# A two-layer graph network on one core: the product with the kept probabilities waits group by group, and the first step's features are added by POOL

## The chip, the cores and the metric

The kernel is one program on one core of one Trainium2 chip. The metric is the device time of one execution in microseconds (us); where several runs of a kernel are given, the median is taken. Five engines work side by side: PE (TensorE: matmuls and turns of tiles), DVE (VectorE), ACT (ScalarE), POOL (GpSimd) and SP (SyncE, which here only issues DMAs). They meet through semaphores alone: an engine that waits stops in its own order of instructions, and everything behind the waiting instruction stops with it.

## What is computed

The input is x of 3327 x 256 and an adjacency matrix of 3327 x 3327. A first layer normalises x and averages it over neighbours. A second layer takes two diffusion steps. What matters here is the second layer:

```python
Rf = S / S.sum(axis=1);  Rb = S / S.sum(axis=0)      # S = adj + I
Xf, Xb, Xa = (X, X, X);  Z = 0
for s in range(2):
    A = adj_from_feats(Xa, W1, W2, W3)    # softmax of Xa W1 W2 (Xa W3)^T, cut to the top 0.9 of
                                          # each row's mass, and softmax again
    Xf = Rf @ Xf;  Xb = Rb @ Xb;  Xa = A @ Xa
    Z = Z + (Xf @ U1[s] + Xb @ U2[s] + Xa @ U3[s])
Y = X + Z                                 # then layer norm, gamma, beta, and the residual
```

So Y begins with X: the features are added once, in the first step (s = 0); the second step adds to what the first left.

## The kernel before

The 3327 rows are 26 tiles of 128 (NT = 26, the last one partly filled). After the first layer the kernel makes two passes, s = 0 and s = 1, here called the first and the second pass. Each goes over the 26 tiles, and a step t of a pass handles one tile of rows. The engines run their own loops and are staggered:

- **DVE** (`step`, from L1376) selects: it evaluates cuts over the 3327 exponentials of tile t (L1150), copies logits of later tiles out of PSUM (L1135), ranks the candidates (L1280 to L1310), and raises a flag for each row whose ranking was not enough (`astray`, L1310). The flags of 128 rows must come into one row to be reduced. SP does that with a small DMA to `flags_row` (L455). Meanwhile DVE writes the first half of the kept values into `window` (L1331), then waits for the DMA, reduces the flags (L1406), writes the second half (L1331), and computes kept_inv (L1457), on which `probs_ready` is set. If a row was flagged, a longer loop runs first.
- **PE** (`step`, from L884) first computes early logits of tile t + 2 (L860; they need `q_tile`, which SP loads), then waits for `probs_ready`, turns `window` in seven groups (L894, P_GROUPS: six of 4 tiles and one of 2) through two PSUM banks, with late logits in between, multiplies the turned groups in `probs_t` with the features `xcur` into `pv_ps` (L903), turns the diffused features (L909), runs the diffusion of tile t + 1 (L880), in which at k = 20 it turns the kept features `ht` (L868), projects the next queries and keys in the first pass (L825), and updates y: in the first pass the features enter `pv_ps` through a product with the identity (L920), in the second pass the y of the first enters in the same way (L923), and then twelve matmul instructions add the three products with U (L926). The end of L926 sets `y_done`.
- **ACT** moves the turned groups from PSUM to `probs_t` (L702, sets `p_moved`), computes exponentials and the first cuts of tile t + 2 (L649 to L678), scales `pv_ps` into `ht` (L711), writes the diffused features to `xfb` and `both` (L689 to L694), and copies `pv_ps` to `y_tile` (L731, sets `y_out`). In the first pass it stores `y_tile` to `y_dram` (the scratch y_scratch) itself, right behind the copy (L733), and waits for the store of the step before ahead of the next copy.
- **POOL** in the passes does only `low_parts` (L536): per step of the first pass one subtraction of 128 x 512.
- **SP** (`load`, L450) does for each step, in this order: the two halves of `q_tile` for tile t + 2 (after logits t), the flags of step t (after DVE's flag), the S tile of step t + 1, and in the second pass the y tile, after `y_done[1]`.

Several semaphores start above zero (`free_slots`): `y_done` and `y_out` at 1, `fb_ready` at 1, `lo_ready` at 1, `s_done` at 2. So in the second pass SP's wait for `y_done[1] >= t + 1` asks for the update of step t - 1.

The wait that the first part of the change splits is one line ahead of the product: `pe.wait_ge(p_moved[s], (t + 1) * NG)`, with NG = 7. Ahead of the flips of group g >= 2, PE already waits until group g - 2 is moved, since the PSUM bank is needed again.

Of the kernel before, what the change touches and what calls it, by code (L numbers as in the profile page):

```python
# [13 lines left out]
P = 128  # L14
N = 3327
D = 256
# [60 lines left out]
def graph_layers(nc, x, adj, w0, b0, w1, w2, w3, u1, u2, u3, gamma, beta, out):  # L77
    ctx = ExitStack()
    with ctx:
# [219 lines left out]
        s_done = [sem(f"s_done_{n}") for n in range(2)]  # L299
        fb_ready = [sem(f"fb_ready_{n}") for n in range(2)]  # L300
        fb_turned = [sem(f"fb_turned_{n}") for n in range(2)]
        lo_ready = [sem(f"lo_ready_{n}") for n in range(2)]
        logits_used = [sem(f"logits_used_{n}") for n in range(2)]
        p_flipped = [sem(f"p_flipped_{n}") for n in range(2)]
# [37 lines left out]
        def tile_of(m, b):  # L342
            return m + HALF_T * b
# [43 lines left out]
        def _(sp):  # L387
# [44 lines left out]
            for s in range(2):  # L432
                def load_q(m, b):
                    for h in range(2):
                        sp.dma_start(q_tile[b][DA * h:DA * (h + 1), :], dram_tile(q_dram[s], tile_of(m, b))).then_inc(q_in[s][b], DMA)
                if s == 0:
                    for b in range(2):
                        sp.wait_ge(team_stored[b], DMA * stores_of(NTEAM + (NTEAM + b) % 2))
                else:
                    sp.wait_ge(q_stored[1], DMA * (NT + 1))  # L440
                for b in range(2):
                    load_q(0, b)

                def load_s(t, m, b):
                    sp.wait_ge(s_done[s], t + 1)
                    sp.dma_start(flat(s_tile[b][:, :, :]), dram_tile(s_dram, tile_of(m, b))).then_inc(s_in[s][b], DMA)

                load_s(0, 0, 0)

                def load(t, m, b):  # L450
                    if not (isinstance(t, int) and t >= NT - 2):
                        sp.wait_ge(logits_ready[s], (t + 1) * NL)
                        load_q(m + 1, b)
                    sp.wait_ge(flags_ready[s], t + 1)
                    sp.dma_start(flags_row, astray[:, :]).then_inc(flags_in[s], DMA)  # L455
                    if not is_last(t):
                        load_s(t + 1, m + b, 1 - b)
                    if s == 1:
                        sp.wait_ge(y_done[1], t + 1)
                        sp.dma_start(y_in[:, :], dram_tile(y_dram, tile_of(m, b))).then_inc(y_loaded[1], DMA)  # L460
                tiles_loop(sp, load)
                if s == 0:

                    for b in range(2):
                        sp.wait_ge(xa_stored[0][b], DMA * (NT // 2 + 1))
                    sp.wait_ge(y_stored[0], DMA * (NT + 1))
                    sp.wait_ge(y_done[0], NT + 1)
                    sp.dma_start(xcur[:, :, :], xa_dram.rearrange("t p d -> p t d")).then_inc(xa_in, DMA)
                    load_u(1)
# [11 lines left out]
        def _(pool):  # L481
# [54 lines left out]
            def low_parts(t, m, b):  # L536
                pool.wait_ge(fb_ready[0], t + 2)
                G.tensor_tensor(tile4(both, tile_of(m, b), 1), xfb[:, :], tile4(both, tile_of(m, b), 0), ALU.subtract).then_inc(lo_ready[0], 1)
            tiles_loop(pool, low_parts)

        @block.scalar
        def _(act):
# [99 lines left out]
            for s in range(2):  # L642
# [54 lines left out]
                def step(t, m, b):  # L697
                    more = not (isinstance(t, int) and t >= NT - 2)

                    for g, (k0, n) in enumerate(P_GROUPS):  # L700
                        act.wait_ge(p_flipped[s], t * NG + g + 2)
                        A.activation(probs_t[:, k0 * P:(k0 + n) * P], flip_ps[g % 2][:, 0:n * P], ACT.Copy).then_inc(p_moved[s], 1)  # L702

                    if more:
                        exponentials(t + 2, b)
                        refine(b, 0)

                    act.wait_ge(pv_done[s], t + 1)
                    if s == 0:
                        act.wait_ge(xa_stored[0][b], DMA * (m + 1))  # L710
                    A.activation(ht[b][:, :], pv_ps[:, 0:D], ACT.Copy, scale=kept_inv[b]).then_inc(xa_ready[s], 1)  # L711
                    if more:
                        refine(b, 1)
                    act.drain()
                    act.wait_ge(fb_turned[s], t + 2)
                    if s == 0:
                        act.wait_ge(xa_ready[0], t + 3)
                        act.dma_start(dram_tile(xa_dram, tile_of(m, b)), ht[b][:, :]).then_inc(xa_stored[0][b], DMA)
                    act.wait_ge(x_turned[s], t + 1)
                    A.activation(flat(xfbt[:, :, :]), flip_ps[1][:, :], ACT.Copy)  # L720
                    A.activation(flat(xt[:, :, :]), pv_ps[:, D:2 * D], ACT.Copy).then_inc(x_t_ready[s], 1)
                    if s == 0:
                        query_key(t, m, b)
                    if not is_last(t):
                        diffused(t + 1, m + b, 1 - b)
                    if s == 0:
                        store_query(t, m, b)
                    act.wait_ge(y_done[s], t + 2)
                    if s == 0:
                        act.wait_ge(y_stored[0], DMA * (t + 1))  # L730
                        A.activation(y_tile[:, :], pv_ps[:, 0:D], ACT.Copy).then_inc(y_out[0], 1)  # L731
                        act.wait_ge(y_out[0], t + 2)
                        act.dma_start(dram_tile(y_dram, tile_of(m, b)), y_tile[:, :]).then_inc(y_stored[0], DMA)  # L733
                    else:
                        A.activation(tile3(y_all, tile_of(m, b)), pv_ps[:, 0:D], ACT.Copy).then_inc(y_out[1], 1)
                for t in range(2):
# [9 lines left out]
        def _(pe):  # L746
# [104 lines left out]
            for s in range(2):  # L851
# [32 lines left out]
                def step(t, m, b):  # L884
# [13 lines left out]
                            logits(t + 2, b, m + 2, [LOGITS_LATE[LATE_AFTER.index(g)]])  # L898

                    pe.wait_ge(y_out[s], t + 1)  # L900
                    pe.wait_ge(p_moved[s], (t + 1) * NG)
                    for k in range(NT):
                        last = T.matmul(pv_ps[:, 0:D], probs_t[:, k * P:(k + 1) * P], xcur[:, k, :], start=(k == 0),  # L903
                                        stop=(k == NT - 1))
                    last.then_inc(pv_done[s], 1)

                    pe.wait_ge(fb_ready[s], t + 2)
# [8 lines left out]
                    if s == 0:  # L916
                        query_key(b)

                    if s == 0:
                        T.matmul(pv_ps[:, 0:D], ident[:, :], tile3(xcur, tile_of(m, b)), start=True, stop=False)  # L920
                    else:
                        pe.wait_ge(y_loaded[1], DMA * (t + 1))
                        T.matmul(pv_ps[:, 0:D], ident[:, :], y_in[:, :], start=True, stop=False)  # L923
                    for j, turned_part in enumerate((xfbt[:, 0:DC, :], xfbt[:, DC:2 * DC, :], xt[:, :, :])):
                        for c in range(DC):
                            last = T.matmul(pv_ps[:, 0:D], turned_part[:, c, :], u_sb[:, j, c, :], start=False,  # L926
                                            stop=(j == 2 and c == DC - 1))
                    last.then_inc(y_done[s], 1)
                    if s == 0:
# [589 lines left out]
```

## Time and profile before

| | us |
|---|---|
| median of 3 runs | 2281.59 (2280.49 to 2283.03) |
| profiled execution, own time | 2276.97 |
| its span, first to last instruction | 2275.3 |
| PE busy | 1915.2 (84%) |
| DVE busy | 1710.6 (75%) |
| ACT busy | 1232.0 (54%) |
| POOL busy | 84.9 (4%) |

The mean granted TensorE clock is 0.940 of full speed. The first pass runs from about 404 to 1209 us, the second from about 1220 to 2218 us. In the first pass an ordinary step lasts 29.2 us, in the second 36.6 us.

How to read the rows further down: times are us from the start of the span. A row of the view in order of time gives start, duration, engine, line, operation, output and input tiles and a count, and in brackets how long the engine was idle before and what ended that. A matmul on 32-bit floats counts as two instructions. PEld is the load of weights, SPq and ACTq are the queues that issue DMAs. A granted clock of 1.00 is 2.4 GHz, 0.50 is 1.2 GHz.

### The profile page before, as it was taken

What the parts mean: (1) busy time and instruction counts of PE and PEld (TensorE: products, weight loads), DVE (VectorE), ACT (ScalarE), POOL (GpSimd) and SP (SyncE); (2) the same over time, 40 slices, a digit from 0 to 9 for tenths busy, and PEclk for the clock granted to TensorE, in tenths of its full rate; (3) what the DMA queues carried; (4) which work ended last, traced back from release to release, by engine and by line L of the source; (5) the groups of instructions that cost most, each with busy time, mean ns of one, the idle gap of its engine ahead of it and who ended that gap; (6) DMA issues with size and microseconds to landing.
All of it is one profiled execution on the core that took longest, in us unless ns stands there. A gap on an engine that the chain in (4) does not pass through costs nothing.

```text
span 2275.3 us, 38276 instructions
## 1 busy us (share of the span) xinstructions
PE 1915.2 (84%) x12364; PEld 1432.6 (63%) x12364; DVE 1710.6 (75%) x4468; ACT 1232.0 (54%) x1922; POOL 84.9 (4%) x141
## 2 busy tenths in 40 slices
PE   4999944899999999995855499999989999999980
PEld 3999922677777777774753356566665656566660
DVE  4222255888888888888861888888889888888957
ACT  4222245566666666663613667576666767575620
POOL 3000020000000000000000000000000000000000
PEclk9999967899999999997978699999999999999995
DMA  6888620111111111110103010101101010101103
GB/s 159 181 177 173 159 82 27 39 43 43 43 43 43 43 43 43 43 43 21 41 6 98 19 38 18 37 18 37 33 22 37 18 37 18 37 18 37 32 6 124
DMA packets 59325, 123.91 MB, mean 54 GB/s; under 512 B 13587, under 2 KB 45713, under 8 KB 59024
## 3 DMA queue, kind: packets, MB, share of 16 engines
q1 hardware_dynamic: 45968, 93.58, 12.0%
q0 software_dynamic: 3744, 22.14, 6.3%
q10 hardware_dynamic: 9568, 7.67, 1.1%
q8 instruction: 18, 0.29, 0.1%
q14 instruction: 27, 0.22, 0.0%
HBM read 107.99 MB, written 37.49 MB: 64 GB/s over the span
## 4 chain that ended last, share of the span: by engine, by line
PE 45%; DVE 31%; DVEq 12%; issue 6%; ACT 3%; DMA 1%; SPq 0%; ACTq 0%; POOL 0%; POOLq 0%
PE bank L903 13%; PE bank L880 6%; DVE stats L1280 5%; PE bank L894 5%; DVE window L1150 5%; PE lg L860 4%; DVE scraps L1150 4%; PE bank L805 4%; PE lg L805 3%; DVEq L1455 3%; PE bank L926 3%; DVEq L1327 2%; DVE window L1323 2%; PE bank L786 2%; DVE sorted_e L1289 1%
## 5 line engine op out<-in xcount | busy, mean ns | idle before, releaser
L903 PE MATMUL bank<-xcur,probs_t 128*128 128x256 f32 x2704 | 597.4, 381 | 37.9 <-ACT probs_t L702 37.9
L903 PEld LDWEIGHTS bank<-xcur,probs_t 128*128 128x128 f32 x2704 | 509.5, 190 | 117.5 <-ACT probs_t L702 47.0
L702 ACT ACTIVATE probs_t<-bank 128x512 f32<-128x512 f32 (+1 forms) x364 | 190.5, 565 | 308.9 <-PE bank L894 308.8
L894 PE MATMUL bank<-ident,window 128*128 128x128 f32 x1352 | 207.7, 297 | 150.7 <-DVE kept_inv L1457 138.6
L894 PEld LDWEIGHTS bank<-ident,window 128*128 128x128 f32 x1352 | 156.2, 149 | 252.8 <-DVE kept_inv L1457 162.4
L880 PE MATMUL bank<-both,s_tile 128*128 128x512 f16 x1352 | 300.1, 379 | 0.0
L1135 DVE TENSOR_SCALAR_CACHE_REDUCE expo<-lg 128x1024 f32 (+1 forms) x208 | 204.9, 1022 | 80.3 <-PE lg L860 63.3
L668 ACT ACTIVATE turned<-expo,found 128x3327 uint8<-128x3327 f32 x78 | 239.6, 3072 | 5.4
L649 ACT ACTIVATE expo<-expo,neg_max 128x3327 f32<-128x3327 f32 x52 | 159.7, 3070 | 152.6 <-DVE neg_max L1144 152.4
L666 ACT ACTIVATE turned<-expo,found 128x3327 uint8<-128x3327 f32 x78 | 239.3, 3068 | 3.8 <-issue 0.2
L860 PE MATMUL lg<-k_t,q_tile 64*128 64x512 f32 (+1 forms) x832 | 201.3, 584 | 44.7 <-DMA q_tile<-q_scratch 23.3
L1280 DVE MAX8 stats<-window 128x8 f32<-128x208 f32 (+1 forms) x780 | 238.8, 383 | 0.0
L880 PEld LDWEIGHTS bank<-both,s_tile 128*128 128x128 bf16 x1352 | 132.1, 98 | 148.3
L1150 DVE SCALAR_TENSOR_TENSOR window<-expo,mine 128x3327 f32 (+1 forms) x54 | 198.9, 3684 | 5.6 <-issue 4.1
L1150 DVE SCALAR_TENSOR_TENSOR scraps<-expo,mine 128x3327 uint8 (+1 forms) x52 | 191.4, 3682 | 0.0
L880 PE MATMUL bank<-parts,s_tile 128*128 128x256 f16 x1352 | 155.9, 273 | 0.0
L860 PEld LDWEIGHTS lg<-k_t,q_tile 64*128 64x128 f32 x832 | 72.0, 198 | 113.8 <-issue 84.8
L926 PE MATMUL bank<-u_sb,turned 128*128 128x256 f32 x624 | 143.2, 379 | 0.0
L880 PEld LDWEIGHTS bank<-parts,s_tile 128*128 128x128 bf16 x1352 | 132.2, 98 | 14.8
L926 PEld LDWEIGHTS bank<-u_sb,turned 128*128 128x128 f32 x624 | 118.6, 190 | 16.1
L1331 DVE SCALAR_TENSOR_TENSOR window<-window,below,expo 128x3327 f32<-128x3327 f32 x28 | 103.1, 3683 | 2.4
L1331 DVE SCALAR_TENSOR_TENSOR window<-expo,below 128x1663 f32 (+3 forms) x52 | 101.3, 1948 | 4.3 <-issue 4.1
(246 smaller groups left out, 2196.3 us busy)
## 6 DMA issues: line engine op xcount, KB each, us to landing
s_tile<-s_scratch SPq DMA_DIRECT2D x52, 832.0 KB, 4.6
expo<-in_adj POOLq DMA_DIRECT2D x25, 831.8 KB, 9.1
s_scratch<-s_tile SPq DMA_DIRECT2D x14, 832.0 KB, 9.0
s_scratch<-probs_t SPq DMA_DIRECT2D x6, 832.0 KB, 9.2
s_scratch<-window SPq DMA_DIRECT2D x6, 832.0 KB, 9.0
x_scratch<-both SPq DMA_DIRECT2D x1, 3328.0 KB, 9.5
q_tile<-q_scratch SPq DMA_DIRECT2D x104, 32.0 KB, 3.2
xa_scratch<-ht ACTq DMA_DIRECT2D x26, 128.0 KB, 1.7
```

The lines of the kernel that those rows point to most:

```text
L666: A.activation(unused, expo[b][:, 0:N], ACT.Sign, scale=-1.0, bias=tried[b][r], accum_out=signs[:, :])
L668: A.activation(unused, expo[b][:, 0:N], ACT.Relu, scale=-1.0, bias=tried[b][r], accum_out=lack[:, :])
L702: A.activation(probs_t[:, k0 * P:(k0 + n) * P], flip_ps[g % 2][:, 0:n * P], ACT.Copy).then_inc(p_moved[s], 1)
L860: last = T.matmul(lg[c % 2][:, h * CHUNK:h * CHUNK + w], q_tile[b][DA * h:DA * (h + 1), :], k_all[DA * h:DA * (h + 1), s, c0:c0 + w], star ...
L880: last = T.matmul(s_ps[:, 0:width], s_tile[b][:, k, :], src[:, k, part, :], start=(k == 0 and part == 0), stop=(k == NT - 1 and part == 1))
L894: last = T.transpose(flip_ps[g % 2][:, k * P:(k + 1) * P], window[:, (k0 + k) * P:(k0 + k + 1) * P], ident[:, :])
L903: last = T.matmul(pv_ps[:, 0:D], probs_t[:, k * P:(k + 1) * P], xcur[:, k, :], start=(k == 0), stop=(k == NT - 1))
L926: last = T.matmul(pv_ps[:, 0:D], turned_part[:, c, :], u_sb[:, j, c, :], start=False, stop=(j == 2 and c == DC - 1))
L1135: V.tensor_scalar(exps_of_halves(b, c0, c0 + w), lg[c % 2][:, :].rearrange("p (h n) -> p h n", h=2)[:, :, 0:w], 1.0, None, ALU.mult, ALU.m ...
L1150: V.scalar_tensor_tensor(out=out, in0=exps(b, 0, N), scalar=cut, in1=exps(b, 0, N), op0=ALU.is_lt, op1=ALU.mult, accum_out=under[:, :])
L1280: V.max(out=best[:, w * 8:(w + 1) * 8], in_=window[:, w * way:(w + 1) * way])
L1331: V.scalar_tensor_tensor(out=window[:, c0:c1], in0=window[:, c0:c1] if ties else exps(b, c0, c1), scalar=below[:, :], in1=exps(b, c0, c1), ...
```

## The change

It has two parts.

1. PE's product with the kept probabilities no longer waits for all seven moved groups ahead of its first matmul. It goes through the groups, and ahead of the last two it waits for the group in question. This holds for both passes.
2. In the first pass the identity's product with `xcur` (L920) is left out, and the first product of L926 starts the sum. ACT copies y without the features into `y_tile` as before. POOL, behind `low_parts(t)`, waits for that copy, adds `xcur`'s tile to `y_tile` and sets the new semaphore `x_added`, which starts at zero. The store of `y_tile` moves from ACT's queue to SP's: in `load`, behind the load of the next S tile, SP waits for `x_added >= t + 1` and issues the store.

```diff
@@ sync, load(t, m, b)
                     if not is_last(t):
                         load_s(t + 1, m + b, 1 - b)
+                    if s == 0:
+                        sp.wait_ge(x_added, t + 1)
+                        sp.dma_start(dram_tile(y_dram, tile_of(m, b)), y_tile[:, :]).then_inc(y_stored[0], DMA)
@@ gpsimd, low_parts(t, m, b)
                 pool.wait_ge(fb_ready[0], t + 2)
                 G.tensor_tensor(tile4(both, tile_of(m, b), 1), xfb[:, :], tile4(both, tile_of(m, b), 0), ALU.subtract).then_inc(lo_ready[0], 1)
+                pool.wait_ge(y_out[0], t + 2)
+                G.tensor_tensor(y_tile[:, :], y_tile[:, :], tile3(xcur, tile_of(m, b)), ALU.add).then_inc(x_added, 1)
@@ scalar, step(t, m, b)
                         A.activation(y_tile[:, :], pv_ps[:, 0:D], ACT.Copy).then_inc(y_out[0], 1)
-                        act.wait_ge(y_out[0], t + 2)
-                        act.dma_start(dram_tile(y_dram, tile_of(m, b)), y_tile[:, :]).then_inc(y_stored[0], DMA)
@@ tensor, step(t, m, b)
                     pe.wait_ge(y_out[s], t + 1)
-                    pe.wait_ge(p_moved[s], (t + 1) * NG)
-                    for k in range(NT):
-                        last = T.matmul(pv_ps[:, 0:D], probs_t[:, k * P:(k + 1) * P], xcur[:, k, :], start=(k == 0),
-                                        stop=(k == NT - 1))
+                    for g, (k0, n) in enumerate(P_GROUPS):
+                        if g >= NG - 2:
+                            pe.wait_ge(p_moved[s], t * NG + g + 1)
+                        for k in range(k0, k0 + n):
+                            last = T.matmul(pv_ps[:, 0:D], probs_t[:, k * P:(k + 1) * P], xcur[:, k, :], start=(k == 0),
+                                            stop=(k == NT - 1))
@@ tensor, step, the update of y
-                    if s == 0:
-                        T.matmul(pv_ps[:, 0:D], ident[:, :], tile3(xcur, tile_of(m, b)), start=True, stop=False)
-                    else:
+                    if s == 1:
                         pe.wait_ge(y_loaded[1], DMA * (t + 1))
                         T.matmul(pv_ps[:, 0:D], ident[:, :], y_in[:, :], start=True, stop=False)
...
-                            last = T.matmul(pv_ps[:, 0:D], turned_part[:, c, :], u_sb[:, j, c, :], start=False,
+                            last = T.matmul(pv_ps[:, 0:D], turned_part[:, c, :], u_sb[:, j, c, :], start=(s == 0 and j == 0 and c == 0),
```

## Rows read from the trace of the kernel before

**Rows 1.** Busy time by stretch: us, then busy us (count) per engine, clock, DMA.
```profile
600.00:1000.00 400.00, 386.08 (x2339) 309.68 (x2337) 343.56 (x864) 252.75 (x425) 16.18 (x14) 1.00 0.13 42
...
1440.00:1900.00 460.00, 427.23 (x2094) 286.00 (x2093) 411.87 (x1116) 309.79 (x431) 0.00 (x0) 0.99 0.08 27
```

**Rows 2.** In order of time, PE, one step of the first pass.
```profile
903.13 1.09 PE L894 MATMUL bank<-ident,window 128*128 128x128 f32 x8
...
909.19 11.49 PE L903 MATMUL bank<-xcur,probs_t 128*128 128x256 f32 x52 [0.74 <-ACT probs_t L702]
...
925.32 0.38 PE L868 MATMUL bank<-ident,ht 128*128 128x128 f32 x2
...
927.29 0.60 PE L920 MATMUL bank<-xcur,ident 128*128 x2
...
927.73 2.75 PE L926 MATMUL bank<-u_sb,turned 128*128 128x256 f32 x12
...
930.41 1.99 PE L860 MATMUL lg<-k_t,q_tile 64*128 64x512 f32 x8
...
932.33 1.09 PE L894 MATMUL bank<-ident,window 128*128 128x128 f32 x8
```

**Rows 3.** In order of time, the same step: DVE, ACT and POOL.
```profile
902.39 1.22 DVE L1135 TENSOR_SCALAR_CACHE_REDUCE expo<-lg 128x1024 f32 x1 [1.46 <-PE lg L860]
...
924.49 0.47 ACT L711 ACTIVATE ht<-bank,kept_inv 128x256 f32<-128x256 f32 x1
...
927.29 0.27 DVE L1406 TENSOR_REDUCE odd_n<-scraps 1x1 int32<-1x128 f32 x1
...
929.02 0.63 ACT L694 ACTIVATE both<-xfb 128x512 f32 x1 [0.15 <-issue]
...
929.86 1.16 POOL L538 TENSOR_TENSOR both<-xfb,both 128x512 f32 x1 [27.84 <-ACT both L694]
929.87 0.16 DVE L1457 RECIPROCAL kept_inv<-cells 128x1 f32 x1 [0.18 <-issue]
...
930.52 0.38 ACT L731 ACTIVATE y_tile<-bank 128x256 f32<-128x256 f32 x1 [0.87 <-PE bank L926]
```

**Rows 4.** In order of time, PE, flips of one step of the second pass.
```profile
1616.51 1.09 PE L894 MATMUL bank<-ident,window 128*128 128x128 f32 x8 [2.27 <-DVE kept_inv L1457]
```

**Rows 5.** In order of time, SP's queue in the step of rows 2.
```profile
925.31 0.53 SPq L455 DMA_DIRECT2D scraps<-astray  x1
926.09 0.39 SPq L446 DMA_DIRECT2D s_tile<-s_scratch  x1
926.77 1.14 SPq L435 DMA_DIRECT2D q_tile<-q_scratch  x2
```

**Rows 6.** In order of time, POOL early in the kernel, then DVE and POOL near 398.
```profile
21.83 2.56 POOL L520 TENSOR_TENSOR parts<-both,parts 128x256 f16<-128x256 f32 x4 [2.70 <-ACT parts L557]
...
396.94 1.94 DVE L1331 SCALAR_TENSOR_TENSOR window<-expo,below 128x1663 f32 x1
...
398.00 1.89 POOL L538 TENSOR_TENSOR both<-xfb,both 128x512 f32 x1 [47.72 <-ACT both L694]
```

**Rows 7.** DMA issues, KB, median to landing: 600 to 1000, the last 350 to 362.
```profile
q_tile<-q_scratch SPq DMA_DIRECT2D x28, 32.0 KB, 3.6
...
scraps<-astray SPq DMA_DIRECT2D x14, 0.5 KB, 2.0
...
q_tile<-q_scratch SPq DMA_DIRECT2D x4, 32.0 KB, 2.1
```

**Rows 8.** Around two pauses of PE: stretches of 1 us, and PE's restarts.
```profile
376.00:377.00 1.00, 0.00 (x0) 0.00 (x0) 0.63 (x4) 0.13 (x1) 0.00 (x0) 0.57 0.00 0
...
383.22 3.54 PE L860 MATMUL lg<-k_t,q_tile 64*128 64x512 f32 x8 [9.86 <-DVE expo L1135]
...
1073.71 2.92 PE L894 MATMUL bank<-ident,window 128*128 128x128 f32 x12 [24.52 <-DVE kept_inv L1457]
...
1079.00:1080.00 1.00, 1.00 (x10) 0.83 (x8) 1.00 (x2) 0.41 (x1) 0.00 (x0) 0.86 0.00 0
```

More of the change, by code:

```diff
@@ L301, in graph_layers @@
         fb_turned = [sem(f"fb_turned_{n}") for n in range(2)]
+        x_added = sem("x_added")
         lo_ready = [sem(f"lo_ready_{n}") for n in range(2)]
```

## The prediction

> **What bounds the kernel now.** I read the table of busy times by stretch first, then one step of each pass in order of time, then SP's own queue. In the first pass (s = 0) PE is busy 386 of 400 us at a granted clock of 1.00, that is at 2.4 GHz, and DVE 344; in the second pass PE has 427 of 460 and DVE 412 [rows 1]. A first-pass step lasts 932.33 - 903.13 = 29.20 us from flips to flips. PE works through flips of the kept weights, their product with the features (L903), the diffusion, the turning of the kept features, query_key, and the update (L920, L926), and goes straight on to the early logits of the step after next [rows 2]. Its only visible stop there is the 0.74 us before L903, for ACT's moves of turned groups. DVE is one step ahead: its kept_inv for step t+1 is ready at 930.03, 2.3 us before PE uses it at 932.33 [rows 2, 3]. So **PE sets the first pass**. In the second pass PE waits 2.27 us for kept_inv ahead of its flips [rows 4]; there **DVE sets the pace**: the list of waits of that pass has none of DVE for another engine.
>
> **Call the end of the update y_done**: 927.73 + 2.75 = 930.48 [rows 2]. Note when the flags of the next selection are made and sent: SP issues them at 925.31, as soon as DVE has them, and DVE's reduction reads them at 927.29 [rows 3, 5]. That is 3.2 us before y_done, so the flags' round trip lies wholly beside PE's work. Everything below turns on this.
>
> **Part 1: L903 waits group by group.** Groups 0 to 4 are known to be moved, since the flips two groups later waited for them; the waits for groups 5 and 6 now stand ahead of k = 20 and k = 24, when some 20/26 of 11.49 us have gone by [rows 2]. So the 0.74 us goes: 26 x 0.74 = 19 us in the first pass if PE stays the bound. What is late next is the turning of the kept features at 925.32: it needs ht, which ACT finishes at 924.49 + 0.47 = 924.96 [rows 2, 3]. That leaves 0.36 us, so of the 0.74 only 0.36 would be gained with the rest unchanged. In the second pass the gain turns into more waiting for kept_inv; only its last two steps, which no selection follows, can give it back: about 1.3 us.
>
> **Part 2: the identity's product leaves PE.** L920 starts at 927.29 and L926 at 927.73, so it holds PE for 0.44 us [rows 2], 11 us over 26 steps. The first product of L926 now starts the sum in its place; that adds no instruction.
>
> **Part 3: POOL's add.** For 128x256, four such operations of L520 take 2.56 us in a row, 0.64 each [rows 6]; the 128x512 one at L538 takes 1.16 and is the upper bound [rows 3], 0.4 (half of it, less its start) the lower. I take 0.64. POOL's low_parts(t) stands ahead of it and was done a step earlier; low_parts(t+1) stands behind it and nobody needs it for 29 us. One L538 took 1.89 us instead of 1.16, at 398.00, while DVE was in a product with two SBUF inputs (396.94 to 398.88) [rows 6]. The Trainium skill (SBUF — State Buffer, on the contention between the engine ports) says that such a DVE operation and a GpSimd one exclude each other for a whole instruction. By that rule the add would wait up to one take_above half, 1.95 us, some 49 us in all, if DVE were then at work; that row agrees with the rule. Here DVE will be idle when the add runs (part 4), so I take nothing for it.
>
> **Part 4: the store and its new wait on SP.** This is the large term. x_added has no free slot, unlike y_done[1] in the second pass, so x_added >= t+1 means that y of this very step is complete. Queued behind it on SP are load_q for step t+3 and **the flags of step t+1**; behind the latter stands DVE's second take_above half, kept_inv, and PE's flips. SP used to issue those flags 5.2 us before y_done; now it can't before y_done(t) has gone through ACT, POOL and the store's issue. From y_done = 0:
> - ACT's copy of y starts 0.04 later and takes 0.38: 0.42 [rows 3]. ACT to POOL takes 0.21 (929.65 to 929.86): 0.63. The add: 1.27. POOL to SP: the trace doesn't show it; PE to ACT took 0.04, ACT to POOL 0.21. I take 0.10: 1.37.
> - SP: from a tile transfer's issue to the next queue entry's 0.68, the q pair 1.14, and a gap of 0.25 as between flags and s_tile [rows 5]; plus 0.15, an estimate for the loop's turn. The flags go out at 3.6.
> - They land 2.0 us later [rows 7], and with 0.1 to DVE the reduction starts at 5.7. From it to kept_inv's end is 929.87 + 0.16 - 927.29 = 2.74, and 0.05 to PE: **flips at 8.5 at the earliest**.
> - The early logits of PE wait for q as well. Its second half is issued at 2.8 and lands 2.1 us (queue otherwise empty) to 3.6 us later (beside an s_tile load) [rows 7]: 4.9 to 6.4, and I take 5.5. PE is thus idle from 0 to 5.5. In the trace the granted clock fell to 0.5, which is 1.2 GHz, after an idle stretch that began at 373.36; it was there by 376.5 [rows 8]. Eight logits then took 3.54 us, against 1.99. So logits run to 9.05, and **flips start at about 9.05**. After the long pause the clock came back at 1079.3, 5.6 us after PE resumed at 1073.71 [rows 8]. So the first 2 us of flips are slow too, 12 in 2.92 against 8 in 1.09: +0.7 [rows 2, 8].
> - From flips to y_done the step took 930.48 - 903.13 = 27.35. Less 0.74 and 0.44, plus 0.7: 26.87. The new step is 9.05 + 26.87 = **35.9 us, 6.7 more than 29.2**.
>
> Should the clock stay high instead, flips start at 8.5, but DVE's first copy, which began 0.74 before them (902.39), then begins with them, ACT's ht comes 0.7 later, and PE waits 0.7 + 0.74 - 0.36 = 1.1 for it: 8.5 + 26.17 + 1.1 = 35.8. The two meet, so little hangs on the clock. The Trainium skill (TensorE: Matmul & The Clock Gate, on oscillation in real kernels) describes waits for DMA between bursts of matmuls after which every burst starts at the low clock. By that rule each of these steps is of the first kind, 35.9; a warm one is 35.8.
>
> **The sum.** Twenty-two ordinary steps (1 to 21, and 23) x 6.7 = 147.4. Steps 22 and 24 ran the long selection, and PE waited over 24 us for kept_inv [rows 8]; the reduction shifts from -3.2 to +5.7, 8.9 later, nothing of it hidden, less 0.44 and about 0.5: +8.0 for step 22. For step 24, which loads no q (1.1 less): +6.7. Step 25: flips followed y_done at once and now come at 7.3, partly slow: +7.6. Step 0: -1.2. The last y goes through POOL and SP before xcur is reloaded: +1.0. Second pass: -1.3. Together 147.4 + 8.0 + 6.7 + 7.6 - 1.2 + 1.0 - 1.3 = **+168 us**. The profiled execution took 2276.97 (its span 2275.3, 1.7 around it), which gives 2445; it lies 4.6 under the median of 2281.59, so for a median I say 2450.
>
> **Rivals.**
> 1. **q sets the restart.** If q lands at 6.4 or later and the logits are slow, flips start at 9.9 to 10.4 and a step is 1 to 1.4 longer: 2475 to 2485. For it: 3.6 us to landing in the ordinary steps [rows 7]. Against: there an 832 KB load runs beside it, here the queue holds only 128 KB of y.
> 2. **SP isn't held** (the other side; the change would do less than I read). If the wait were met a step earlier, by a count that is one ahead, the flags go out as now and the store hides. Then the first pass gains 0.44 and 0.36 per step: 26 x 0.8 = 21 us, 2260. It decides from the point where x_added(t) comes before DVE has the flags of t+1, that is 5.2 us before y_done. Against it: the add can't start before y exists.
> 3. **Cheap hops.** POOL at 0.4, issues back to back, flags in 1.9: flips at 7.4, high clock, ht on time: 5.3 per step, 2415.
>
> **How the numbers follow.** Forecast 0.80; rival 1 0.12; rival 3 0.04; rival 2 0.03; and 0.01 for no difference by some cancellation. The range from 2415 to 2487 takes in the forecast's bounds (5.3 to 8.2 per step) and rival 1, and leaves out rival 2 and a tail above. About 0.2%, 4.6 us, is what a measurement of this kernel can tell from no change: faster 0.03, same 0.01, slower 0.96.
>
> **What would show it.** In the changed trace: first-pass flips every 35 to 37 us; SP issuing the flags 3 to 4 us after y_done, directly behind y's store and the q pair; DVE's reduction waiting for their DMA, 8 us or more per step where it waited none; PE waiting for q some 5 us; granted clock below 1.00 in the first pass; the wait before L903 gone in both passes, and in the second pass about 3.0 us instead of 2.27 before the flips, with its step unchanged. I am wrong if SP issues the flags before y_done, or if the first pass keeps its 29 us. If the period is right but flips follow kept_inv and not the logits, then q was quicker than I took it.

## The result and the profile after

The changed kernel takes **2444.2 us** (median of 4, 2443.48 to 2444.63) against 2281.1: ratio **1.0713, 95% interval 1.0695 to 1.0732**. In the medians that is 163 us more. The prediction was 2450. The profiled execution took 2443.48, which is 166.5 more than the profiled one of before, where the sum said 168; the profiled one of before was 4 us under the median of its kernel. One execution of a later kernel (early moves, below) took 4340 us and is left out of its median.

Busy time in the same two stretches as in [rows 1] (us, then per engine PE, PEld, DVE, ACT, POOL busy us and count, granted clock, DMA share, GB/s), kernel after:

```profile
600.00:1000.00 400.00, 335.77 (x1888) 258.72 (x1887) 281.88 (x711) 210.82 (x346) 20.15 (x22) 0.91 0.10 33
...
1440.00:1900.00 460.00, 417.63 (x2033) 280.30 (x2034) 411.12 (x1105) 298.52 (x421) 0.00 (x0) 0.95 0.09 30
```

In the first pass PE is no longer full: 336 us of 400 instead of 386. DVE has 282 instead of 344, since fewer steps fall into the same 400 us, and the clock is 0.91. In the second pass DVE's 411 us of 460 is unchanged, and the clock is 0.95 instead of 0.99.

One first-pass step in order of time, kernel after; it answers to [rows 2, 3, 5]:

```profile
1003.48 0.44 PE L872 MATMUL bank<-ident,ht 128*128 128x128 f32 x2 [0.84 <-ACT ht L717]
...
1005.63 2.76 PE L930 MATMUL bank<-u_sb,turned 128*128 128x256 f32 x12
...
1008.42 0.38 ACT L737 ACTIVATE y_tile<-bank 128x256 f32<-128x256 f32 x1 [0.29 <-PE bank L930]
1008.99 0.72 POOL L544 TENSOR_TENSOR y_tile<-y_tile,xcur 128x256 f32<-128x256 f32 x1 [34.24 <-ACT y_tile L737]
1009.67 1.15 POOL L542 TENSOR_TENSOR both<-xfb,both 128x512 f32 x1
1009.88 0.36 SPq L461 DMA_DIRECT2D y_scratch<-y_tile  x1
1010.54 1.23 SPq L436 DMA_DIRECT2D q_tile<-q_scratch  x2
1011.83 0.58 SPq L456 DMA_DIRECT2D scraps<-astray  x1
...
1013.64 3.78 PE L864 MATMUL lg<-k_t,q_tile 64*128 64x512 f32 x8 [5.26 <-DMA q_tile<-q_scratch]
1013.83 0.27 DVE L1410 TENSOR_REDUCE odd_n<-scraps 1x1 int32<-1x128 f32 x1 [8.26 <-DMA scraps<-astray]
...
1016.41 0.16 DVE L1461 RECIPROCAL kept_inv<-cells 128x1 f32 x1 [0.18 <-issue]
...
1017.36 2.46 PE L898 MATMUL bank<-ident,window 128*128 128x128 f32 x12
...
1022.96 11.39 PE L909 MATMUL bank<-xcur,probs_t 128*128 128x256 f32 x52
...
1039.20 0.44 PE L872 MATMUL bank<-ident,ht 128*128 128x128 f32 x2
```

Read it from y_done = 1005.63 + 2.76 = 1008.39. Before, the flags were issued 5.2 us ahead of y_done. Here they are issued at 1011.83, 3.4 us behind it, and the rows between show why: SP waited for ACT's copy and POOL's add, then issued y's store and the q pair, and only then the flags. DVE then sits idle for 8.26 us at L1410, where [rows 3] has no wait. From one turning of ht to the next the step lasts 1039.20 - 1003.48 = 35.7 us. Over steps 1 to 20 the mean, from start to start of the product L909, is 35.84 against 29.20. Steps of 36.0 and 35.7 alternate, so such a mean depends by some 0.05 on the point that it is taken at (from turning to turning of ht it is 35.9). The means below are taken at the product too.

The waits between 600 and 1000 us, kernel after (engine, line, waited for: us in total, times, longest):

```profile
DVE odd_n L1410 <- DMA scraps<-astray: 91.3, 11, 8.4
...
PE lg L864 <- DMA q_tile<-q_scratch: 57.7, 11, 5.4
```

Both are in every one of the eleven steps: DVE waits 8.3 us for its flags, PE 5.2 us for q. The DMA issues of the same stretch say how long q took from issue to landing (KB, median us), 2.0 instead of the 3.6 of [rows 7]. In [rows 5] q goes out right behind the S tile's load, here long behind it:

```profile
q_tile<-q_scratch SPq DMA_DIRECT2D x22, 32.0 KB, 2.0
```

Where the 166.5 us lie: the first pass, from SP's first q load to its reload of xcur, took 1021.8 us instead of 857.7, so +164.1. The second pass took 1007.8 instead of 1006.8, and what is ahead of the first pass ended 1.5 us later.

### The profile page after: what moved, and what is told of

Read it like the earlier page. It is cut to its first block, busy times and chain, and to the rows that moved or that the text cites. A ratio compares the mean times of both kernels' runs of the same rounds, so it can differ in the third digit from the quotient of the medians.

```text
span 2441.8 us, 38266 instructions
## 1 busy us (share of the span) xinstructions
PE 1964.4 (80%) x12312; PEld 1448.3 (59%) x12312; DVE 1712.8 (70%) x4468; ACT 1233.4 (51%) x1922; POOL 101.9 (4%) x167
## 4 chain that ended last, share of the span: by engine, by line
DVE 31%; PE 31%; DVEq 12%; ACT 12%; issue 8%; DMA 3%; SPq 2%; POOL 1%; ACTq 1%; POOLq 0%
DVE scraps L1154 7%; PE lg L864 6%; DVE stats L1284 5%; DVE window L1154 4%; PE bank L898 4%; PE bank L909 4%; PE bank L809 3%; PE lg L809 3%; PE bank L930 3%; PE bank L884 3%; DVEq L1459 3%; ACT turned L672 3%; ACT turned L674 3%; ACT expo L655 3%; DMA q_tile<-q_scratch 2%
## 5 line engine op out<-in xcount | busy, mean ns | idle before, releaser
L909 PE MATMUL bank<-xcur,probs_t 128*128 128x256 f32 x2704 | 592.2, 379 | 0.0
L909 PEld LDWEIGHTS bank<-xcur,probs_t 128*128 128x128 f32 x2704 | 509.7, 190 | 67.1
L864 PE MATMUL lg<-k_t,q_tile 64*128 64x512 f32 (+1 forms) x832 | 249.4, 709 | 166.9 <-DMA q_tile<-q_scratch 145.1
L898 PE MATMUL bank<-ident,window 128*128 128x128 f32 x1352 | 223.8, 314 | 174.0 <-DVE kept_inv L1461 166.7
L898 PEld LDWEIGHTS bank<-ident,window 128*128 128x128 f32 x1352 | 170.6, 160 | 299.1 <-DVE kept_inv L1461 217.8
L864 PEld LDWEIGHTS lg<-k_t,q_tile 64*128 64x128 f32 x832 | 85.3, 232 | 251.5 <-issue 218.9
L1410 DVE TENSOR_REDUCE odd_n<-scraps 1x1 int32<-1x128 f32 (+1 forms) x52 | 14.2, 274 | 207.2 <-DMA scraps<-astray 207.2
```

What stands on the lines that cost most here:

```text
L864: last = T.matmul(lg[c % 2][:, h * CHUNK:h * CHUNK + w], q_tile[b][DA * h:DA * (h + 1), :], k_all[DA * h:DA * (h + 1), s, c0:c0 + w], star ...
L898: last = T.transpose(flip_ps[g % 2][:, k * P:(k + 1) * P], window[:, (k0 + k) * P:(k0 + k + 1) * P], ident[:, :])
```

## The experiments

The first kernels ask whether the wait on SP is the loss, or POOL's add, or the store's new queue.

**Store from ACT again.** POOL still adds; only the queue and thereby the waiting engine differ.

```diff
@@ sync
-                    if s == 0:
-                        sp.wait_ge(x_added, t + 1)
-                        sp.dma_start(dram_tile(y_dram, tile_of(m, b)), y_tile[:, :]).then_inc(y_stored[0], DMA)
@@ scalar
                         A.activation(y_tile[:, :], pv_ps[:, 0:D], ACT.Copy).then_inc(y_out[0], 1)
+                        act.wait_ge(x_added, t + 1)
+                        act.dma_start(dram_tile(y_dram, tile_of(m, b)), y_tile[:, :]).then_inc(y_stored[0], DMA)
```

> The changed kernel, but the first pass's y tile is stored from ACT's queue again, behind POOL's add (ACT waits for x_added), so SP has no new wait. Theory (the place of the wait on SP is the whole loss): the flags go out 5.2 us before the end of the update again and a first-pass step is 29.2 less 0.44 (identity's product) less 0.36 (what ht's arrival leaves of the 0.74), so 28.4 us; 26 x 0.8 = 21 us under the kernel before, 2260 us (2255 to 2266). Rival (POOL's add or the longer way of y through POOL is the loss): the time stays above 2300.

Measured: 2263.5 us, 0.9921 of before (0.9904 to 0.9937). A step lasts 28.66 us. The loss of 163 us is gone and a gain of 18 is there. In order of time, that kernel:

```profile
916.24 0.53 SPq L456 DMA_DIRECT2D scraps<-astray  x1
...
920.80 0.38 ACT L734 ACTIVATE y_tile<-bank 128x256 f32<-128x256 f32 x1 [0.44 <-PE bank L929]
921.37 0.72 POOL L541 TENSOR_TENSOR y_tile<-y_tile,xcur 128x256 f32<-128x256 f32 x1 [26.72 <-ACT y_tile L734]
...
922.12 0.34 ACTq L736 DMA_DIRECT2D y_scratch<-y_tile  x1
```

The flags go out at 916.24, 4.6 us ahead of the copy of y. POOL's add is as long as in the changed kernel. Only ACT waits for it, until it issues the store at 922.12, and that is ahead of ACT's first move of a turned group (923.31).

**Store on SP, one step later.** In this kernel x_added starts at 1, so the same wait asks for the add of step t - 1. The store stands behind the flags and ahead of the S tile's load. The diff doesn't show that start, the last tile's store behind the loop, and the wait's first turn, which lets one store out that a later one overwrites.

```diff
@@ sync, load(t, m, b)
                     sp.dma_start(flags_row, astray[:, :]).then_inc(flags_in[s], DMA)
+                    if s == 0:
+                        sp.wait_ge(x_added, t + 1)
+                        sp.dma_start(dram_tile(y_dram, tile_of(m, 0) if b else m - 1 + HALF_T), y_tile[:, :]).then_inc(
+                            y_stored[0], DMA)
...
-                    if s == 0:
-                        sp.wait_ge(x_added, t + 1)
-                        sp.dma_start(dram_tile(y_dram, tile_of(m, b)), y_tile[:, :]).then_inc(y_stored[0], DMA)
```

> The changed kernel with the store still on SP, but SP waits for the add of step t-1, behind the flags of step t and ahead of the S tile's load; the last tile is stored behind the loop, and one extra store of a tile that is overwritten later stands in for the semaphore's free count. Theory: SP waits for something that was complete some 20 us before, the flags aren't held, and the time is that of the kernel with ACT's store, 2260 us, within 3 us of it. Rival (the store on SP costs time wherever it stands, through the queue): above 2290.

Measured: 2263.4 us (0.9920, 0.9903 to 0.9936), 28.67 per step. It is the same as with ACT's store. So the queue isn't the cause either; what SP's wait asks for, at its place ahead of q and the flags, is. (The store also moved ahead of the S tile's load; that alone was not tried.)

**Part 2 alone, and the store's place alone.** The first puts the old wait for all groups back. The second keeps the store on SP, but puts the identity's product back on PE and takes POOL's add away (the diff is the second's):

```diff
@@ sync
-                        sp.wait_ge(x_added, t + 1)
+                        sp.wait_ge(y_out[0], t + 2)
@@ gpsimd
-                pool.wait_ge(y_out[0], t + 2)
-                G.tensor_tensor(y_tile[:, :], y_tile[:, :], tile3(xcur, tile_of(m, b)), ALU.add).then_inc(x_added, 1)
@@ tensor
-                    if s == 1:
+                    if s == 0:
+                        T.matmul(pv_ps[:, 0:D], ident[:, :], tile3(xcur, tile_of(m, b)), start=True, stop=False)
+                    else:
...
-                            last = T.matmul(pv_ps[:, 0:D], turned_part[:, c, :], u_sb[:, j, c, :], start=(s == 0 and j == 0 and c == 0),
+                            last = T.matmul(pv_ps[:, 0:D], turned_part[:, c, :], u_sb[:, j, c, :], start=False,
```

> Part 2 alone: POOL's add and SP's store, with the old wait for all groups ahead of the product. Theory: the stall is all of part 2; without part 1 PE comes 0.74 us later to the turning of the kept features, where the changed kernel waits for ht some 0.5 us, so a step is 0.25 us longer: 2444 + 6 = 2450 us (2446 to 2456). Rival (the two parts work together in the loss): clearly under 2440.

Measured: 2457.3 us (1.0772, 1.0741 to 1.0803), a step 36.23. That is a little above the range that was expected.

> The changed kernel with the identity's product back on PE and without POOL's add: SP stores y behind ACT's copy. Theory: the place of the store on SP costs nearly all by itself; the chain loses ACT to POOL, the add and POOL to SP, 1.1 us per step, and PE gets 0.44 back onto its path: 2444 - 25 x 1.1 + 26 x 0.44 = 2428 us (2420 to 2434). Rival (POOL's add is the loss): 2270 to 2300.

Measured: 2433.1 us (1.0666, 1.0635 to 1.0697), a step 35.41. The store's place on SP costs nearly all of it with no add on POOL at all. It is 5 us more than the 2428 expected. Of these, 25 x 0.17 = 4 are the way from ACT to SP (ACT's copy ends at 1001.27 + 0.38, SP issues at 1001.82), which I had taken for nothing. Part 2 alone lost 7 us more than expected; what of that is understood comes below, with part 1.

**Is each thing on that way counted once per step?** A second addition on POOL, and, in another kernel, the q loads moved ahead of SP's wait:

```diff
@@ gpsimd (second addition)
                 pool.wait_ge(y_out[0], t + 2)
+                G.tensor_tensor(idle[:, :], y_tile[:, :], tile3(xcur, tile_of(m, b)), ALU.add)
                 G.tensor_tensor(y_tile[:, :], y_tile[:, :], tile3(xcur, tile_of(m, b)), ALU.add).then_inc(x_added, 1)
@@ sync (q first; not shown: load_q is gone from its old place in the first pass, and the load of step 0 stands ahead of the loop)
                     if s == 0:
+                        if not isinstance(t, int):
+                            sp.wait_ge(logits_ready[0], (t + 2) * NL)
+                            load_q(m + b + 1, 1 - b)
                         sp.wait_ge(x_added, t + 1)
```

> The changed kernel with a second POOL addition of the same size, into a tile nobody reads, ahead of the one that counts. Theory: POOL's add lies on the step's path from the update to the flags, so its start-to-start time of some 0.65 us comes on top in each of 25 steps: 2444 + 16 = 2460 us (2457 to 2464). Rival (the path has slack behind the q load or the low clock): under 2452.

Measured: 2460.4 us (1.0786, 1.0764 to 1.0808); 36.53 per step, 0.69 more. In the medians it is 16.2 us, or 0.65 for each of 25 steps; in the rows the second addition starts 0.67 us behind the first:

```profile
1019.73 0.72 POOL L545 TENSOR_TENSOR idle<-y_tile,xcur 128x256 f32<-128x256 f32 x1 [34.30 <-ACT y_tile L739]
1020.40 0.72 POOL L546 TENSOR_TENSOR y_tile<-y_tile,xcur 128x256 f32<-128x256 f32 x1
```

> The changed kernel with the q loads of the first pass ahead of SP's wait for x_added instead of behind the store. Theory: PE's early logits follow the update at once, and the flags go out 1.25 us earlier (the time of the two issues); since kept_inv leads the rest of the step, each of about 24 steps is 1.25 us shorter: 2444 - 30 = 2414 us (2408 to 2420). Rival (PE's wait for q sets the step, and the flags are hidden behind it): 2 or more us per step, under 2395.

Measured: 2412.2 us (1.0574, 1.0543 to 1.0605), 34.53 per step, 1.31 less. In order of time, that kernel:

```profile
1021.58 1.99 PE L871 MATMUL lg<-k_t,q_tile 64*128 64x512 f32 x8
...
1023.98 0.54 SPq L460 DMA_DIRECT2D scraps<-astray  x1
...
1025.96 0.27 DVE L1417 TENSOR_REDUCE odd_n<-scraps 1x1 int32<-1x128 f32 x1 [6.94 <-DMA scraps<-astray]
...
1028.76 2.92 PE L905 MATMUL bank<-ident,window 128*128 128x128 f32 x12 [5.20 <-DVE kept_inv L1468]
```

PE waits for q no more and runs its logits at once at full speed. Yet the step loses only about the time of the q pair's issue (1.23 us in the rows of the kernel after), since PE now waits 5.20 us for kept_inv instead. **The flags set the step, not q.**

**The clock.** PE is kept busy inside the stall:

```diff
@@ tensor, behind the update of the first pass
                         pe.wait_ge(qk_out, t + 2)
+                        for k in range(0 if is_last(t) else 9):
+                            T.matmul(flip_ps[1][:, 0:D], ident[:, :], xcur[:, k, :], start=True, stop=True, skip_group_check=True)
```

> The changed kernel, and behind each first-pass update but the last PE does nine products with the identity whose result nobody reads, some 4 us, inside its wait for q. Theory: the granted clock stays at 1.00 through the stall, logits and flips run at full speed, but the way DVE's copies, ACT's exponentials, ht is as long as before from kept_inv on and now PE waits longer for ht: no change, 2444 us (2440 to 2447). Rival (the low clock is on the path): 0.7 to 1.5 us per step less, 2406 to 2426.

Measured: 2442.8 us (1.0709, 1.0677 to 1.0740), 35.90 per step (from turning to turning of ht 35.9, as in the kernel after). The clock does what it was meant to. The kernel after, two single microseconds, then this kernel's stretch and one turning of ht:

```profile
1011.00:1012.00 1.00, 0.00 (x0) 0.00 (x0) 0.00 (x0) 0.00 (x0) 0.00 (x0) 0.94 0.22 69
...
1018.00:1019.00 1.00, 1.00 (x7) 0.85 (x5) 1.00 (x4) 0.49 (x1) 0.00 (x0) 0.65 0.00 0
```

```profile
600.00:1000.00 400.00, 355.33 (x2085) 286.72 (x2084) 281.75 (x711) 210.19 (x346) 20.23 (x22) 1.00 0.10 33
...
1016.69 1.09 PE L898 MATMUL bank<-ident,window 128*128 128x128 f32 x8 [1.19 <-DVE kept_inv L1463]
...
1039.26 0.44 PE L872 MATMUL bank<-ident,ht 128*128 128x128 f32 x2 [1.24 <-ACT ht L717]
```

In the kernel after the clock fell from 2.4 to 1.2 GHz at 1011.9, while PE stood idle, was 0.50 in every microsecond between, and came back at 1018.7, during the flips. With PE kept busy it is 1.00 over the whole stretch. Flips then start 0.67 us earlier (1016.69 against 1017.36), PE waits 1.24 us for ht at L872, and the turning happens at the same time, 1039.26 against 1039.20. From kept_inv on, the step runs by DVE's copies, ACT's exponentials and ht; the slow clock lay beside that.

**Part 1 alone.**

```diff
@@ tensor, kernel before
-                    pe.wait_ge(p_moved[s], (t + 1) * NG)
-                    for k in range(NT):
...
+                    for g, (k0, n) in enumerate(P_GROUPS):
+                        if g >= NG - 2:
+                            pe.wait_ge(p_moved[s], t * NG + g + 1)
+                        for k in range(k0, k0 + n):
...
```

> The kernel before with part 1 alone, the waits group by group. Theory: PE comes 0.74 us earlier to the turning of the kept features, ht leaves it 0.36 of that; 26 x 0.36 = 9 us and about 1 in the second pass's last steps: 2271 us (2268 to 2274). Rival (PE is the bound at every place and ht is hidden): 26 x 0.74 = 19 and 1: 2261. Rival (nothing is gained, DVE sets the first pass): 2281.

Measured: 2272.4 us (0.9960, 0.9946 to 0.9974), inside what was expected. But the way to it is another, and that the total fits is partly luck: an ordinary step is 29.09 us, only 0.11 less and not 0.36. Step 0 and the step behind the first long selection gain the whole 1.0 (28.19 and 28.2), and the first pass is 7.0 us shorter in all, of which the ordinary steps give 2 to 3. In order of time, that kernel:

```profile
906.55 0.87 PE L894 MATMUL bank<-ident,window 128*128 128x128 f32 x6
907.26 11.39 PE L905 MATMUL bank<-xcur,probs_t 128*128 128x256 f32 x52
918.49 0.60 PE L911 MATMUL bank<-ident,xfb 128*128 128x128 f32 x4
...
924.00 0.44 PE L868 MATMUL bank<-ident,ht 128*128 128x128 f32 x2 [0.55 <-ACT ht L711]
...
925.09 0.38 ACT L721 ACTIVATE turned<-bank 128x256 f32<-128x256 f32 x1
925.59 0.65 PE L825 MATMUL bank<-turned,wqk 128*128 128x128 f32 x4
```

From the last flips to the turning of xfb it is 918.49 - 906.55 = 11.94 us. The same two points in the kernel before are 12.94 apart:

```profile
907.57 0.87 PE L894 MATMUL bank<-ident,window 128*128 128x128 f32 x6
...
920.51 0.60 PE L909 MATMUL bank<-ident,xfb 128*128 128x128 f32 x4
```

So the wait was worth **1.00 us**, not the 0.74 that stands as idle time. Without it the product starts at 907.26, 0.16 before the flips' end as it is written (ends of matmuls are modelled), and takes 11.39 instead of 11.49. Of that 1.00 PE gives 0.70 back ahead of ht: from the turning of xfb to that of ht it is 924.00 - 918.49 = 5.51 us, where it was 925.32 - 920.51 = 4.81. The row writes 0.55 of that as idle. Another 0.1 to 0.2, different from step to step, goes behind it: ht's transposes take 0.44 instead of 0.38 here, ACT's second move (L721) ends at 925.47, and L825 comes right behind. The kernel with ACT's store and the old wait takes the two parts apart:

> As the kernel with ACT's store, but with the old wait for all moved groups: part 2 alone without SP's wait. Theory: the identity's product alone is worth its 0.44 us per step, 26 x 0.44 = 11: 2270 us (2268 to 2273), and the group waits were worth the rest of the way to 2263. Rival (the copies' order on ACT takes back part of it too): 2275 or more.

Measured: 2272.1 us (0.9957, 0.9940 to 0.9974), 28.76 per step: 0.44 less than 29.20, as read from the rows. So POOL's add and ACT's wait for it cost nothing here.

**What ACT's order holds back.** Three kernels build on the one with ACT's store. ACT's step in the first pass runs: exponentials, a first and a second pass over them for the cut (L666, L668), small steps, ht, moves of the turned features.

Here kept() is ht with its waits, and moves() the moves of the turned features. The first argument of refine behind the 0 is called between the two passes over the exponentials, the second behind the second pass. `early` holds in the first pass, but for its last two steps.

```diff
@@ scalar, step: early ht
+                    def kept():
+                        act.wait_ge(pv_done[s], t + 1)
...
                     if more:
                         exponentials(t + 2, b)
-                        refine(b, 0)
+                        refine(b, 0, kept if early else None)
...
@@ early moves, in place of that; both_of calls kept() and moves()
-KEPT_AT = 20
+KEPT_AT = (12, 20)
...
+                        refine(b, 0, both_of if early else None)
...
@@ moves behind, in place of that
-KEPT_AT = 20
+KEPT_AT = (16, 20)
...
+                        refine(b, 0, kept if early else None, moves if early else None)
```

The kernel with early moves also writes the output of its second pass, which nobody reads, into probs_t instead of turned.

> As the kernel with ACT's store, and ACT also makes ht in the first pass between the two passes over the exponentials instead of behind both. Theory (ht is what took the rest of the 0.74): PE no longer waits for ht and the full 0.74 + 0.44 comes out of each first-pass step: 28.0 us, 26 x 1.18 = 31 and 1: 2249 us (2244 to 2254). Rival (something else than ht held the turning): no different from the kernel with ACT's store, about 2260.

Measured: 2261.0 us (0.9906, 0.9890 to 0.9923), 28.50 per step, and the time is on the rival's side: 2.5 us under the kernel with ACT's store, not 14. Its reason isn't the rival's, though: PE waits for ht no more, but the next thing from ACT is late. In order of time:

```profile
909.82 0.48 ACT L713 ACTIVATE ht<-bank,kept_inv 128x256 f32<-128x256 f32 x1
...
915.80 0.38 ACT L729 ACTIVATE turned<-bank 128x256 f32<-128x256 f32 x1
...
916.23 0.71 PE L833 MATMUL bank<-turned,wqk 128*128 128x128 f32 x4 [0.40 <-ACT turned L729]
```

> As the kernel with ACT's store and the early ht, and ACT also moves the turned kept features in the first pass between its two passes over the exponentials; PE turns them at k = 12 of the diffusion instead of 20. In the kernel with the early ht alone PE no longer waits for ht but 0.40 us for that move (L729), which stands behind ACT's second pass. Theory (ACT's order is what keeps the 0.74 us from being gained): an ordinary first-pass step goes from 28.5 to 28.0 us, 26 x 0.5 = 13 under 2261, less what ACT's later work gives back: 2249 us (2246 to 2254). Rival (DVE is the next bound, or ACT is late for the end of the step): 2258 or more.

Measured: 2267.8 us (0.9937, 0.9918 to 0.9957), 28.76 per step, the rival's side. With the moves between the two passes, ACT stands idle for 2.80 us ahead of them until PE has turned ht. So the second pass ends late, and PE stands still at the step's end, for the copies of query and key:

```profile
916.93 0.60 ACT L722 ACTIVATE turned<-bank 128x512 f32<-128x512 f32 x1 [2.80 <-PE bank L883]
...
920.65 0.20 ACT L673 ACTIVATION_READ_ACCUMULATOR probs_t<-expo,found 128x1 f32 x1
...
922.58 0.27 ACT L607 ACTIVATE q_stage<-bank 64x128 f32<-64x128 f32 x1
...
923.53 1.99 PE L875 MATMUL lg<-k_t,q_tile 64*128 64x512 f32 x8 [0.54 <-issue]
```

The view calls that idle time "issue", but the program has PE wait there for qk_out, which ACT sets at 922.58 + 0.27 = 922.85, when the update is all but through, so that nothing behind it could be made ready. That is my reading of the program and wasn't tested by itself.

> As the kernel with ACT's store and the early ht, and ACT moves the turned kept features in the first pass directly behind its second pass over the exponentials, ahead of the small steps of the cut; PE turns them at k = 16. The kernel that moved them between the two passes had PE wait 0.54 us at the step's end, since the second pass then ran until 920.8 and the copies of query and key came late. Theory (ACT has one place in its order where neither the move nor the end of the step is late): 28.0 us per ordinary step, 2249 us (2246 to 2254). Rival (ACT's order can't give both): 2258 or more.

Measured: **2245.0 us, 0.9840 of before (0.9827 to 0.9854)**, 1 us under the range that was expected. It is 27.76 in every ordinary step, where 28.0 had been expected: 29.20 less 0.44 less 1.00. PE's rows show none of the stops any more:

```profile
911.97 0.88 PE L907 MATMUL bank<-ident,window 128*128 128x128 f32 x6
912.68 11.39 PE L918 MATMUL bank<-xcur,probs_t 128*128 128x256 f32 x52
923.91 0.60 PE L924 MATMUL bank<-ident,xfb 128*128 128x128 f32 x4
...
927.84 0.38 PE L881 MATMUL bank<-ident,ht 128*128 128x128 f32 x2
...
930.24 0.61 PE L838 MATMUL bank<-turned,wqk 128*128 128x128 f32 x4
930.69 2.76 PE L939 MATMUL bank<-u_sb,turned 128*128 128x256 f32 x12
933.37 1.99 PE L873 MATMUL lg<-k_t,q_tile 64*128 64x512 f32 x8
```

Both halves of the change are in this kernel. It beats the one before by 37 us in the medians, with the store off the way of the flags.

## Why the prediction was right, point by point

- **What bounds the kernel**: right. PE set the first pass, DVE the second. (The 0.74 us wasn't PE's only visible stop in the first: its flips also wait 0.25 us for ACT, at 904.47, which neither part changes.) In the second pass nothing moved (1007.8 us against 1006.8). The wait ahead of the flips grew less than forecast. Over the same 18 steps it is 41.2 us instead of 32.7, so 2.3 on average instead of 1.8; it varies from step to step, between 1.6 and 3.3 after and between 0.7 and 2.3 before, and 2.27 in [rows 4] was one of the longest. One of the longest after, in a step whose flips ran at the low clock:

```profile
1527.35 2.92 PE L898 MATMUL bank<-ident,window 128*128 128x128 f32 x12 [3.24 <-DVE kept_inv L1461]
```

- **The wait on SP is the large term**: right, and shown. Taking it away in two ways gives 2263.5 and 2263.4; with no POOL add but the store on SP the loss stays (2433).
- **The sum**: its large term was right, and that it comes within 2 us of 166.5 is partly luck. For the first pass it had 147.4 + 8.0 + 6.7 + 7.6 - 1.2 + 1.0 = 169.5, and 164.1 was measured. For the rest it had -1.3, and +2.5 was measured. In the medians it was 163 against 168.
- **The way from y_done to the flips**: its hops were sized as they came out. The flags were forecast at 3.6 us after y_done and went out at 3.44; the reduction at 5.7, it came at 5.44; flips at 9.05, they came at 8.97. POOL's add took 0.72 us, not 0.64, well inside the bounds, and counts once per step (a second addition starts 0.67 behind the first, and each step is that much longer, within what the means can tell). Rival 1, q at 6.4 us or later, did not come: PE's logits start 5.25 us after y_done. (The 2.1 us of [rows 7] weren't for an otherwise empty queue, as I had it: an S tile's load was issued right behind those four, at 356.16.)
- **Which of two ways ends last**: here the step was wrong, though the sum wasn't. I took PE's way (q, slow logits, slow flips) for the one that sets the step at 35.9, and the way by kept_inv and ht, 35.8, for the case of a high clock. The runs show the second at work at either clock: with the clock held at 1.00 the time stays (2442.8), with q loaded early the time falls by the flags' share alone (2412.2). The two were 0.1 us apart in the forecast, so the number didn't suffer. For the high clock 1.1 us of waiting for ht was forecast, and PE waits 1.24. On the rule of the Trainium skill (TensorE: Matmul & The Clock Gate, on oscillation in real kernels) that bursts of matmuls after waits for DMA start at the low clock: by that rule the steps were to start slow, and this trace agrees (0.50 from 1011.9 to 1018.7).
- **Part 1's 0.74 us, of which 0.36 would stay**: the right mechanism, both sizes off. The wait was worth 1.00 (12.94 against 11.94), and what ACT leaves of it is 0.11. ht itself leaves 0.30, near the 0.36 that I had read off its arrival (924.96 to 925.32); I had nothing for what is lost behind it, where ACT's second move comes right ahead of L825. The 1.00 also bears on part 2 alone, which lost 7 us more than expected: with the old wait PE comes 1.00 us later, not 0.74, in 25 steps 6.5 us. That accounts for the size, but the rows don't bear it out in full: its ordinary steps are 0.39 us longer than the changed kernel's, about 8 us in all, and some 4 us more lie in steps 22 to 25, which weren't looked into.
- **The identity's 0.44**: right to the digit (28.76 against 29.20).
- **Rival 3's time, and with it the lower end of the range**: wrong as added up. Flips at 7.4 us with ht on time give 7.4 + 26.17 = 33.6 us, 4.4 more than 29.2 and not 5.3. By the forecast's own way of adding, that is some 2390 us and not 2415. The measured time lies above both.
- **The special steps**: steps 22, 24 and 25 grew by 7.3, 5.4 and 6.2 us, not 8.0, 6.7 and 7.6, so 3.4 less together; the second pass gave no 1.3 us back. The reading for these steps, that nothing of the shift is hidden, was a little too strict; which part of it is hidden wasn't looked into.
- **The contention of POOL and DVE**: nothing was taken for it, and the add is 721 to 724 ns in all 26 steps. In the rows above DVE stands idle while it runs, so this case can't speak against the rule.

## What to carry to other kernels

A wait on the engine that issues DMAs is a wait for everything that it issues behind it: before a transfer moves to a queue, write down what stands behind its new place and when that is needed, and compare with when the wait ends, not with the transfer's own deadline. A store that nobody waits for can go one round later, behind the urgent entries, as long as its tile isn't overwritten before (here ACT's next copy waits for it). And where one engine's stop goes, look at every later arrival from the other engines: here three places in ACT's order (ht, the second move, the copies of query and key) each ate part of one microsecond, until all of them stood right.

## What was not expected of the hardware

The idle time in a row understates what a stop of PE costs here: 0.74 us are written beside the product, and without the wait the stretch from flips to the next turning is 1.00 us shorter. The 128x128 transposes of ht take 0.44 us for a pair where PE or its weight load waited for ht (924.00 with part 1 alone), and 0.38 where neither did (925.32 before), both at a granted clock of 1.00. And a granted clock of 0.50 for 6.8 us of a 35.7 us step cost no time that could be measured (2442.8 against 2444.2), since PE wasn't the last to arrive.
